# Two transformer layers on one core: first attention through a band of values, second attention in another order

## The reference

```python
x = x + xattn0(layernorm(x), ctx)   # 16 heads of 16, q and k normalised per head
x = x + moe0(layernorm(x))          # 8 experts, 2 per token, hidden 512
x = x + xattn1(layernorm(x), ctx)   # one head of 256
x = x + moe1(layernorm(x))          # 32 experts, 4 per token, and a shared expert
...
attn = jax.nn.softmax(jnp.einsum('bhqd,bhkd->bhqk', qh, kh), axis=-1)
x = jnp.einsum('bhqk,bhkd->bhqd', attn, vh)
```

## Time and profile before

| | us |
|---|---|
| median of three runs | 1439.91 |
| the profiled execution | 1447.97 |
| its span | 1446.1 |
| first attention, 110.6 to 372 | 261.4 |
| experts of layer 0, 419 to 798 | 379 |
| second attention, 810 to about 930 | 120 |

### The profile page before, as it was taken

The page is one execution under the profiler, slowest core; times in us unless marked ns, Lnnn a source line. Parts: engine busy times, 40 slices in busy tenths (PEclk is TensorE's granted clock), DMA queues, the critical chain, the costliest instruction groups (busy, mean ns, idle before and its releaser), DMA issues. The chain is left out here.

```text
span 1446.1 us, 29159 instructions
## 1 busy us (share of the span) xinstructions
PE 1322.6 (91%) x7743; PEld 1056.2 (73%) x7744; DVE 766.0 (53%) x1965; ACT 594.8 (41%) x1314; POOL 663.6 (46%) x905
## 2 busy tenths in 40 slices
PE   7998999999879999999999599847999999989993
PEld 4665777777558888888888387724888888858882
DVE  4884888887732222222222488693233333347764
ACT  2455777777322222222222377635333333322110
POOL 1213565665113333333332366504555555257775
PEclk9998999999889999999999599966999999999997
DMA  2108322222731111111111677554455555745554
GB/s 96 59 30 307 114 92 89 78 96 100 288 119 48 50 50 51 50 50 51 51 51 37 202 228 218 163 232 155 154 164 161 162 161 156 131 125 161 161 161 126
DMA packets 117387, 179.94 MB, mean 124 GB/s; under 512 B 17210, under 2 KB 91979, under 8 KB 113996
## 3 DMA queue, kind: packets, MB, share of 16 engines
q1 hardware_dynamic: 80980, 100.29, 20.8%
q0 software_dynamic: 20736, 56.65, 14.6%
q10 hardware_dynamic: 15608, 22.25, 4.3%
HBM read 115.13 MB, written 59.77 MB: 121 GB/s over the span
## 5 line engine op out<-in xcount | busy, mean ns | idle before, releaser
L1228 POOL DMA_INDIRECT xg<-t_xn,token x160 | 151.7, 948 | 157.7 <-PE psum L2093 72.8
L2167 POOL DMA_INDIRECT su_yg<-t_y,slot x128 | 125.4, 980 | 67.9 <-issue 38.1
L2105 PE MATMUL psum<-gu,m_xT 128*128 x640 | 154.2, 384 | 0.0
L1465 PE MATMUL psum<-w,m_hT 128*128 x576 | 136.3, 380 | 0.8 <-ACT m_hT L1384 0.8
L1403 DVE TENSOR_TENSOR m_h<-psum,m_h 128x512 f32<-128x512 f32 x72 | 49.8, 691 | 164.8 <-ACT m_h L1378 164.8
L2105 PEld LDWEIGHTS psum<-gu,m_xT 128*128 128x128 f32 x640 | 117.2, 193 | 13.2
L1444 PE MATMUL psum<-w,m_xT_high 128*128 x288 | 120.8, 420 | 0.0
L2064 DVE TENSOR_TENSOR m_h<-psum,m_sg 128x256 f32<-128x256 f32 x80 | 34.0, 425 | 162.0 <-ACT m_sg L2043 161.9
L1444 PE MATMUL psum<-w,m_xT_low 128*128 x288 | 114.9, 399 | 0.0
L1444 PE MATMUL psum<-w_low,m_xT_high 128*128 x288 | 114.2, 396 | 0.0
L1465 PEld LDWEIGHTS psum<-w,m_hT 128*128 128x128 f32 x576 | 103.8, 190 | 12.4 <-issue 1.2
(11 more groups left out here) (305 smaller groups left out, 3126.1 us busy)
## 6 DMA issues: line engine op xcount, KB each, us to landing
t_y<-m_y SPq DMA_DIRECT2D x80, 256.0 KB, 2.2
w<-in_w SPq DMA_DIRECT2D x8, 1024.0 KB, 11.3
t_x<-at_x SPq DMA_DIRECT2D x64, 128.0 KB, 2.1
t_w_low<-at_low ACTq DMA_DIRECT2D x64, 128.0 KB, 1.7
w_low<-t_w_low SPq DMA_DIRECT2D x8, 1024.0 KB, 13.3
at_yg<-t_y SPq DMA_DIRECT2D x32, 256.0 KB, 3.1
gu<-in_gu ACTq DMA_DIRECT2D x8, 1024.0 KB, 11.9
w<-in_x SPq DMA_DIRECT2D x16, 256.0 KB, 2.8
```

The source lines that it names most:

```text
L1228: pool.indirect_dma_start(out=g.xg1[j % GB][:, k * D:(k + 1) * D], out_offset=None, in_=g.xn4, in_offset=bass.IndirectOffsetOnAxis(ap=g.to ...
L1465: last = pe.matmul(ps_y[:, 0:D], hT[:, c * P:(c + 1) * P], g.w2[:, bass.ds(ex * (MC * D) + c * D, D)], start=(c == 0), stop=(c == MC - 1))
L2105: last = pe.matmul(ps_gu[p][:, k * 2 * M1:(k + 1) * 2 * M1], xT[p][:, at:at + P], g.gu[:, bass.ds(ex[k] * (DC * 2 * M1) + c * 2 * M1, 2 * ...
L2167: pool.indirect_dma_start(out=yg[p][k][:, :], out_offset=None, in_=g.y1, in_offset=bass.IndirectOffsetOnAxis(ap=g.slot[:, at:at + 1], axis ...
```

## The change

Four parts, in one edit.

- **Probabilities in pieces, values as a band.** The 616 probability columns of a step are padded to 640 and transposed in 5 pieces of 128 columns, across the borders of heads. Each transposed piece is then held still (128 rows, 128 tokens), and a band of values is streamed: for the 2 or 3 heads that the piece touches, 17 columns each, zero where a row belongs to another head. The bands (204 columns per batch and group of heads) are built once, at the end of the projections, by 24 DMAs from `v_all`, which moves into the space of `w13`. The result comes out in token rows, so L742 and L814 go, and so does the copy of values on POOL (L636). A bfloat16 matmul of zeros (1 row, 272 columns) opens the sum of each tile.
- **Norm on ScalarE.** The layer norm of the first attention is applied by ScalarE (`apply_scalar`, with one more small operation on POOL), one step earlier than on VectorE before; the copies of the best experts are made once in four tiles.
- **One slot less** in the experts of layer 0: 71 for 72. At most 71 can be used, since the slots are 64 full ones and at most one more for each expert but one.
- **Second attention reordered** on TensorE, ScalarE and SyncE.

```diff
-NS0 = NTOK * K0 // P + E0
+NS0 = NTOK * K0 // P + E0 - 1
...
-        pool.wait_ge(self.s_rstd, t.n + 1)
+        wait_alone(pool, self.s_rstd, t.n + 1, self.s_passed[1])
...
+ROWS = HG * LK
+PIECES = -(-ROWS // P)
+
+
+def heads_in(j):
+
+    return range(j * P // LK, (min((j + 1) * P, ROWS) - 1) // LK + 1)
+
+
+BAND_AT = [sum(len(heads_in(i)) for i in range(j)) * (DH + 1) for j in range(PIECES + 1)]
+BAND = BAND_AT[PIECES]
...
+        v_all = g.w13[:, at + 8 * D:at + 8 * D + NB * VW]
...
-            steps(sp, 4, NQP, NQP, 4, load_x)
+            few(4, load_x)
+            sp.wait_ge(s_zero, NG)
+            sp.wait_ge(v_out, NKP)
+            moved = 0
+            for gr in range(NG):
+                for j in range(PIECES):
+                    for i, h in enumerate(heads_in(j)):
+                        first, end = max(h * LK, j * P), min((h + 1) * LK, (j + 1) * P)
+                        to = g.v_band[gr].rearrange("p (b n) -> p b n", n=BAND)
+                        of = v_all.rearrange("p (b n) -> p b n", n=VW)
+                        at_to, at_of = BAND_AT[j] + i * (DH + 1), (gr * HG + h) * (DH + 1)
+                        sp.dma_start(to[first - j * P:end - j * P, :, at_to:at_to + DH + 1],
+                                     of[first - h * LK:end - h * LK, :, at_of:at_of + DH + 1]).then_inc(s_band, 16)
+                        moved += 1
+                    load_x(At(None, 0, 4 + gr * PIECES + j))
+            for t in range(4 + NG * PIECES, NQP):
+                load_x(At(None, 0, t))
+            sp.wait_ge(s_band, moved * 16)
...
-            pool.memset(g.v_all[:, :], 1.0).then_inc(s_v1, 1)
+            pool.memset(v_all, 1.0).then_inc(s_v1, 1)
+            for gr in range(NG):
+                pool.memset(g.v_band[gr], 0.0).then_inc(s_zero, 1)
...
-        T_RAW, T_N, T_O, T_WP, T_X, T_R = 4, 5, 6, 7, 9, 10
+        T_N, T_O, T_WP, T_XA, T_X, T_R = 4, 5, 6, 7, 8, 9
...
-                        wait_alone(pool, pv_mm, b.shift(-1).n * 4, passed[1])
-                        pool.tensor_copy(v_b[bp_][0:LK, :], g.v_all[0:LK, bass.ds(b.n * VW, VW)]).then_inc(v_ready, 1)
...
@@ VectorE @@
-                    dve.wait_ge(raw_t, t.n + 1)
+                    ov = ps_o[p][:, 0:NG * OW].rearrange("p (h d) -> p h d", h=H)
+                    dve.wait_ge(pv_mm, t.n * 2 + 2)
...
-                t = tile_at(u, T_WP + 1)
-                if t is not None:
-                    p = t.mod(2)
-
-                    wait(dve, xn_st[p], t.div(2).n * 16)
-                    wait(dve, x_t, t.shift(-1).n)
-                    ln.apply(dve, x1[p][:, :], xn[p][:, :], t).then_inc(x_norm, 1)
...
+                    top_of(dve, lg[p], top[:, at], ix[:, at], t, lg_done, m8_done, ix_done, passed)
+                    if t.mod(RANKED) == RANKED - 1:
+                        at = bass.ds(t.shift(1 - RANKED).n * 8, RANKED * 8)
+                        dve.tensor_copy(g.top_v[:, at], top[:, :])
+                        wait_alone(dve, ix_done, t.n + 1, passed[0])
+                        dve.tensor_copy(g.top_i[:, at], ix[:, :])
...
@@ ScalarE @@
-                    act.activation(prT[p][0:LK, :].rearrange("p (a k) -> p a k", a=2), ps_tp[0:LK, :, :], ACT.Copy)\
+                    act.activation(prT[p][:, :], ps_tp[:, :, :].rearrange("p a n -> p (a n)")[:, 0:PIECES * P], ACT.Copy)\
...
-                t = tile_at(u, T_RAW - 1)
-                if t is not None:
-                    p = t.mod(2)
-                    act.wait_ge(pv_mm, t.n * 2 + 2)
-
-                    wait(act, raw_t, t.shift(-1).n)
-                    act.activation(oraw[p][:, :], ps_raw, ACT.Copy).then_inc(raw_out, 1)
...
+                t = tile_at(u, T_XA)
+                if t is not None:
+                    p = t.mod(2)
+
+                    wait(act, xn_st[p], t.div(2).n * 16)
+                    wait(act, x_t, t.shift(-1).n)
+                    ln.apply_scalar(act, x1[p][:, :], xn[p][:, :], t).then_inc(x_norm, 1)
...
@@ TensorE @@
-                    for h in range(HG):
-                        last = pe.transpose(ps_tp[0:LK, h // 4, (h % 4) * P:(h % 4 + 1) * P],
-                                            pr[p][:, h * LK:(h + 1) * LK], g.ident[:, :])
+                    if v.loop is None and v.off == 0:
+                        pe.wait_ge(s_tail, 2)
+                    for j in range(PIECES):
+                        last = pe.transpose(ps_tp[:, j // 4, (j % 4) * P:(j % 4 + 1) * P],
+                                            pr[p][:, j * P:(j + 1) * P], g.ident[:, :])
...
-                        wait(pe, raw_out, t.n)
+                        wait(pe, o_norm, t.shift(-1).n)
                         if t.loop is None and t.off == 0:
-                            pe.wait_ge(ps_clear, 1)
-                    for h in range(HG):
-                        c = (gr * HG + h) * (DH + 1)
-                        at, quarter = 32 * (h % 4), 2 * gr + h // 4
-                        last = pe.matmul(ps_raw[at:at + DH + 1, quarter * P:(quarter + 1) * P],
-                                         v_b[b.mod(2)][0:LK, c:c + DH + 1], prT[p][0:LK, h * P:(h + 1) * P], start=True, stop=True)
+                            pe.wait_ge(s_tail, 4)
+                        pe.matmul(ps_o[t.mod(2)][:, 0:NG * OW], one16[:, :], zero16[:, :], start=True, stop=False)
+                    for j in range(PIECES):
+                        n = BAND_AT[j + 1] - BAND_AT[j]
+                        at = gr * OW + heads_in(j)[0] * (DH + 1)
+
+                        last = pe.matmul(ps_o[t.mod(2)][:, at:at + n], prT[p][:, j * P:(j + 1) * P],
+                                         g.v_band[gr][:, bass.ds(b.n * BAND + BAND_AT[j], n)],
+                                         start=False, stop=(gr == NG - 1 and j == PIECES - 1))
                     last.then_inc(pv_mm, 1)
-                t = tile_at(u, T_RAW)
-                if t is not None:
-                    p = t.mod(2)
-                    pe.wait_ge(raw_out, t.n + 1)
-                    wait(pe, o_norm, t.n)
-                    for c in range(4):
-                        last = pe.transpose(ps_o[:, c * P:(c + 1) * P], oraw[p][:, c * P:(c + 1) * P], g.ident[:, :])
-                    last.then_inc(raw_t, 1)
...
@@ second attention, SyncE: one step @@
-                if (t := stage(s, 0)) is not None and not (t.loop is None and t.off < GB):
-                    load(t)
+                if (t := stage(s, XM + 1)) is not None:
+                    p = t.mod(2)
+                    sp.wait_ge(xm_done, t.n + 1)
+                    sp.dma_start(g.xn4[rows(t), :], xm[p][:, :]).then_inc(xm_st[p], 16)
                 if (t := stage(s, WO + 1)) is not None:
                     q = t.mod(4)
                     sp.wait_ge(x3_done, t.n + 1)
                     sp.dma_start(g.x3[rows(t), :], x3[q][:, :]).then_inc(x3_st[q], 16)
-                if (t := stage(s, XM + 1)) is not None:
-                    p = t.mod(2)
-                    sp.wait_ge(xm_done, t.n + 1)
-                    sp.dma_start(g.xn4[rows(t), :], xm[p][:, :]).then_inc(xm_st[p], 16)
+                if (t := stage(s, XM + 2)) is not None:
...
+                if (t := stage(s, 0)) is not None and not (t.loop is None and t.off < GB):
+                    load(t)
...
@@ second attention, ScalarE: the order of one step @@
-                if (t := stage(s, R)) is not None:
...
+                if (t := stage(s, XA)) is not None:
...
-                if (t := stage(s, XA)) is not None:
...
+                if (t := stage(s, R)) is not None:
...
```

More of the change, by code:

```diff
@@ L498, in attention0_phase @@
         NU = NT * NG
[L499 removed]
+        RANKED = 4
+        OW = HG * (DH + 1)
         HW = HG * LK // 2
@@ L1756, in step @@
                     last.then_inc(x_t, 1)
-                if (t := stage(s, XM)) is not None:
-                    p = t.mod(2)
-                    pe.wait_ge(xm_done, t.n + 1)
-                    wait(pe, xm_out, t.n)
-                    for c in range(DC):
-                        last = pe.transpose(ps_m[:, c * P:(c + 1) * P], xm[p][:, c * P:(c + 1) * P], g.ident[:, :])
-                    last.then_inc(xm_t, 1)
                 if (t := stage(s, WO)) is not None:
@@ L1778, in step @@
                         .then_inc(wo_mm, 1)
+                if (t := stage(s, XM)) is not None:
+                    p = t.mod(2)
+                    pe.wait_ge(xm_done, t.n + 1)
+                    wait(pe, xm_out, t.n)
+                    for c in range(DC):
+                        last = pe.transpose(ps_m[:, c * P:(c + 1) * P], xm[p][:, c * P:(c + 1) * P], g.ident[:, :])
+                    last.then_inc(xm_t, 1)
+                if (t := stage(s, R)) is not None:
+                    p = t.mod(2)
+                    pe.wait_ge(xm_out, t.n + 1)
+                    pe.wait_ge(exp_done, NT if t.loop is None and t.off + 5 > NT else t.shift(5).n)
+                    pe.matmul(logits_of(t), ones3[:, :], bias3[:, NB * LK:NB * LK + E1], start=True, stop=False)
```

(4 more changed lines are left out.)

84 lines of the change are left out of this document (37 added, 47 removed).

## The result

The changed kernel takes 1449.5 us (median of 10 runs, 1447.33 to 1458.84) against 1439.97 (10 runs, 1436.26 to 1444.97): ratio 1.0076, 95% interval 1.0052 to 1.0100, slower by 9.5 us. The forecast was 1442.8, in a range of 1429 to 1466. The profiled execution after took 1447.54 us, span 1445.7. Its span is no longer than that of before, because the execution shown of before lies 8 us over its median; the stages tell more.

What follows compares the result with a forecast made beforehand. TensorE's work was taken to bound the steady first attention and layer 0's experts; +1 + 7.0 - 2.6 - 5.2 + 2.7 = +2.9 us, carried to the median of 1439.91, gave 1442.8 us, range 1429 to 1466.

Steps and rivals of the forecast that it cites:

- projections: Projections: 24 band copies take 24 us and delay the loads of x, the first ones by about one: +1 us.
- first attention, steady: First attention, 32 tiles: 3.55 us of TensorE work goes and 3.77 comes, +0.22 us a tile, +7.0 us.
- its end: End of the first attention: one of ten emptying steps of 2.6 us goes, -2.6 us.
- one slot: Experts of layer 0: one slot of 5.22 us of TensorE work goes, nothing takes its place, -5.2 us.
- second attention: Second attention: S held for the logits' copy, +5.7 us, less 3.0 of lost time; +2.7, bounds -4.8 and +9.
- I take 3.0 of the 4.8 as gone: Second attention: 25 steps lose 4.8 us beyond 3.30 each; the reordering was to remove 3.0 of it.
- it still has about a step: Second attention: the load of x and expert outputs, issued nearly a step later, still has about a step to spare.
- a floor: First attention: 0.110 us per matmul holding 128 columns, set by the held side; with it +2.6 us.
- the rival at 1457.5: First attention: register operations on TensorE's queue, ten more a tile, are not hidden; +14.7 us, chance 0.11.
- the first rival: Projections: band copies starve the loads of x; +10.5 us at 36 us of copying, +22 at 48; chance 0.22.
- +11.5: Projections: by the skill's rule the first engine gets 2,658 packets, 36 us, making this part +11.5 instead of +1.
- The second rival: Second attention: no new wait and the bubbles go, new matmuls at 0.110 us; -10 us, 1430 us, chance 0.29.

## Why the prediction was right or wrong

The sign and the range were right; the size was 2.9 us for 9.5, and 1449.5 lies just outside the 1436 to 1449 that the forecast gave itself. By its steps:

| step | forecast | the two profiles | means over all profiles of that stage |
|---|---|---|---|
| projections | +1 | +4.0 | +2.6 (116.2 of eight, 113.6 of three) |
| first attention, steady | +7.0 | +2.3 | +3.3 (237.3 of eleven, 234.0 of three) |
| its end | -2.6 | -3.6 | -3.2 (23.0 of eleven, 26.2 of three) |
| one slot | -5.2 | -6.6 | -6.2 (372.6 of twelve, 378.8 of two) |
| second attention | +2.7 | +8.1 | +13.9 (117.2 of three, 103.3 of four) |
| sum | +2.9 | +4.2 | +10.4; +9.5 by the medians |

Each profile is one execution. So the forecast missed by 11 us in the second attention, and by 4 the other way in the first.

**Second attention: the step that failed.** The forecast's own mechanism, S held by the logits' copy, was right. Its size was 0.22 us a step and 5.7 in all; between the two kernels that differ in the logits' place alone, the last 25 steps differ by 7.6. A plain step is held for 0.24, near the forecast, and one with a register operation behind the wait for 0.39, which the forecast did not have. That the stage as a whole shows 5.8 against the old order is near 5.7 by chance: it is the 7.6 less the bubbles that the order gets rid of. Two sentences beside the mechanism were wrong. "I take 3.0 of the 4.8 as gone": only about 2 us are usually there to win, since four other executions lose 0.6 to 2.9 in those 25 steps, and the run with neither change 0.4. And "it still has about a step" on the load that now leaves last in SyncE's step: it does not, as VectorE's wait for it shows. Worse, the store of the transposed result, which the diff puts a step later, was not costed at all. Its buffers are two, and ScalarE refills one in the very step in which its store is now issued. SyncE's order was in the forecast as a gain, or at nothing; it costs 8 us on top of the held S, and 11 (by the ratios) to 17 (by the one profile) when alone. That the clock would fall behind the longer waits was not in the forecast either.

**First attention.** The price of L837 was taken as 0.117 us from a matmul with 32 columns. It is 1.14 / 10 and 1.04 / 10, 0.114 and 0.104, the second below the 0.110 that was called a floor; and ten transposes cost 1.19 for 1.22. A tile gained 0.03 us by its groups and 0.04 by its pace, for the forecast 0.22: 1.2 us in the steady tiles. The rest of the 2.3 lies in the filling of the pipeline, and the 3.3 of the means holds the executions with a late rise of the clock there. The register operations are hidden, as forecast: the rival at 1457.5 would need 0.46 us a tile more. The end of the stage gained 3.6, a step of 2.6 as forecast and 1.0 more, which no run divides.

**Projections.** The delay has the place that the first rival named, late loads of x: VectorE waits 2.6 to 3.6 us for them in the eight kernels with the copies between them, and never in the others. The last of the ten loads landed at 89.3, forecast for 85. The forecast priced packets on the DMA engines: 13.7 ns (11.6 measured) on 11.2 engines (half of 16 measured), 24 us. What takes 28.5 us is SyncE's queue. Whether SyncE is held there by its own work or by DMA engines that have fallen behind is open. For its own work: an ordinary issue takes about 0.85 us whatever its rows. For the engines: in all ten profiles with copies on SyncE, the four issues of 2.2 to 3.3 us stand right behind a copy of 51 or of 76 rows, be they a copy or a load, with few engines at work. Mean busy shares, of 0.50 or 0.60, do not show that the engines had room.

The rule of the Trainium skill ("DMA: Bandwidth & Descriptors", section "Why a DMA increments its semaphore by 16 and not by 1") comes nearer on the engines: 8 busy on average is less than an even spread, and its 2,658 packets on the first engine at 11.6 ns would be 31 us (an estimate) for the 28.7. By it the copies of 51 and 76 rows are the ones on 3 and 4 engines. But its consequence, +11.5, did not come, since the copies hide all but some 3 us.

**Chances.** Slower had the largest of the three chances, 0.45, but for other reasons: what came is the forecast's case with late DMAs and the clock behind them, which no rival held. The second rival (no new wait, 1430) failed at the held S and at SyncE. Of the signs that the forecast named, the pitch of L837 and the hold of S by about 0.2 us came; a tile of 7.6 to 7.7 us (7.52) and the last of the ten loads by 86 (89.3) did not.

## What to carry to other kernels

When a diff moves DMA issues within a queue's step, work out for each store and load which buffer it frees or fills, how many of them there are, and in which step the next user comes: here what was moved on SyncE cost as much as what was moved on TensorE and ScalarE. DMAs must be priced at the issuing queue as well as at the DMA engines, and by the issue that stands behind each of them. A wait that leaves TensorE idle can cost more than its own length, if the clock falls behind it. And before a gain is taken from the idle time of one profile, ask whether that idle time is there in a second one, and at which clock the stage ran.

## What the runs showed of the hardware

- Issuing a copy in runs of 68 bytes held SyncE for 0.71 to 1.31 us in the kernel with the loads first, with 25 rows as with 77 (400 and 1,232 runs), against 0.37 for a load of 256 runs of 1 KB issued alone. The issue right behind a copy of 51 or 76 rows took 2.2 to 3.3 us in all ten profiles, also where it was a copy of one row or a load. The 24 copies together: 28.5 us on SyncE while the DMA engines were 50% busy on average, and 24 to 41% in the long issues.
- The same copies issued by GpSimd held it for 0.59 to 2.12 us each, 27.5 us together, and it stood idle for 7.4 and 6.5 us ahead of two of them.
- Matmuls that hold 128 columns and stream 34 or 51 follow each other at 0.104 to 0.114 us, like those that stream one at 0.110.
- A register operation behind a wait that is really waited for adds about 0.15 us to the step (3.55 and 3.69 in turn); in the kernel with the logits' own place and SyncE's old step the same operations cost nothing, and the steps with them take 3.30 like the others.
- In the second attention TensorE's granted clock fell from 1.00 to 0.50 for 3.4 us at a time (once for 13.6) behind idle stretches of TensorE of 0.8 to 2.3 us; in the same stage other idle stretches of 1.2 to 1.6 us were not followed by a fall.
- The end of the last stage differed by 60 to 70 us between the profiles shown and the runs of the experiments, for all kernels alike. Its cause was not looked into.
